# Swapping the V product and the t product on TensorE in the attention slots of a gated transformer block

## What is computed

```
q = layernorm(x) @ w_q;  k = ctx @ w_k;  v = ctx @ w_v
x = x + tanh(g_xattn) * softmax(causal(q k^T / sqrt(512))) @ v
x = x + tanh(g_ffn) * (gelu(layernorm(x) @ tern(W1)^T + b1) @ tern(W2)^T + b2)
```

## Time and profile before

| | before |
|---|---|
| runs, us | 1613.87, 1618.36, 1619.16 (median 1618.36) |
| span of the profiled execution, first to last instruction | 1614.5 us, mean granted clock of PE 0.991 |
| busy PE, DVE, ACT, POOL | 1574.7, 1087.3, 811.1, 481.5 us |
| attention stage, from 43 to 766 us | 723.0 us, PE busy 704.5, DVE busy 489.3 |

### The profile page before, as it was taken

The page is one execution under the profiler, slowest core; times in us unless marked ns, Lnnn a source line. Parts: engine busy times, 40 slices in busy tenths (PEclk is TensorE's granted clock), DMA queues, the critical chain, the costliest instruction groups (busy, mean ns, idle before and its releaser), DMA issues.

```text
span 1614.5 us, 26067 instructions
## 1 busy us (share of the span) xinstructions
PE 1574.7 (98%) x10028; PEld 982.1 (61%) x10028; DVE 1087.3 (67%) x1825; ACT 811.1 (50%) x1448; POOL 481.5 (30%) x467
## 2 busy tenths in 40 slices
PE   7799999999999999999989999999999999999998
PEld 4455556565656555555656666666666666666665
DVE  6666657665656679866666677667676677667664
ACT  2333333433233553323656666666666666666664
POOL 3211111111111111133344443345344444345320
PEclk9899999999999999999999999999999999999999
DMA  7445455453646986666222333324222323323110
GB/s 209 111 94 150 104 142 111 113 133 91 153 101 169 222 249 158 150 156 119 63 76 48 97 79 85 78 55 98 76 76 47 98 76 82 74 65 98 50 50 27
DMA packets 307532, 170.81 MB, mean 106 GB/s; under 512 B 268160, under 2 KB 268176, under 8 KB 306128
## 3 DMA queue, kind: packets, MB, share of 16 engines
q1 hardware_dynamic: 306512, 166.78, 42.2%
q10 hardware_dynamic: 720, 2.10, 0.4%
q0 software_dynamic: 176, 0.27, 0.1%
HBM read 70.53 MB, written 33.55 MB: 64 GB/s over the span
## 4 chain that ended last, share of the span: by engine, by line
PE 89%; DVE 4%; issue 2%; ACT 1%; DMA 1%; POOL 0%; SPq 0%; DVEq 0%
PE s_ps L1234 14%; PE e_ps L1234 14%; PE s_ps L1299 11%; PE o_ps L1329 10%; PE v_ps L1280 9%; PE t_ps L1261 8%; PE t_ps L1178 7%; PE o_ps L1178 7%; PE v_ps L1178 7%; PE m_ps L1178 3%; DVE w_s L1074 1%; DMA x_ring<-in_x 1%; DVE negmax L897 0%; PE e_ps L1329 0%; DVE ctx_s L742 0%
## 5 line engine op out<-in xcount | busy, mean ns | idle before, releaser
L1037 DVE SCALAR_TENSOR_TENSOR v_s<-xnT,sc,v_s 128x512 f16<-128x512 f32 x256 | 239.7, 957 | 104.7 <-ACT v_s L667 104.7
L660 ACT ACTIVATE xnT<-tT,b_s 128x256 f32<-128x256 f32 x384 | 173.9, 499 | 178.5 <-DVE tT L1025 62.2
L1234 PE MATMUL s_ps<-w_s,v_s 128*128 128x512 f16 x1024 | 262.8, 379 | 0.0
L1234 PE MATMUL e_ps<-w_s,v_s 128*128 128x512 f16 x1024 | 262.8, 379 | 0.0
L563 ACT ACTIVATE p<-s_ps,ebias,esc 128x128 f32<-128x128 f32 (+3 forms) x64 | 53.2, 831 | 355.7 <-DVE ebias L901 355.7
L1299 PE MATMUL s_ps<-ctx_s,tT 128*128 128x512 f16 (+3 forms) x1152 | 197.7, 326 | 3.7 <-DVE tT L858 3.7
L1329 PE MATMUL o_ps<-v_s,pT 128*128 128x512 f16 x840 | 192.0, 380 | 0.0
L1280 PE MATMUL v_ps<-wv_s,ctx_s 128*128 128x512 f16 x768 | 180.0, 385 | 7.8 <-DVE v_s L865 7.8
L1261 PE MATMUL t_ps<-xnT,a_s 128*128 128x256 f16 x1488 | 176.9, 276 | 8.2 <-issue 7.9
L667 ACT ACTIVATE v_s<-xnT,sc 128x512 f16<-128x512 f32 x256 | 176.2, 712 | 7.5
L1234 PEld LDWEIGHTS e_ps<-w_s,v_s 128*128 128x128 f16 x1024 | 100.2, 98 | 120.8
(11 more groups left out here) (169 smaller groups left out, 2401.5 us busy)
## 6 DMA issues: line engine op xcount, KB each, us to landing
out_y<-x_ring SPq DMA_DIRECT2D x128, 256.0 KB, 2.2
x_ring<-in_x SPq DMA_DIRECT2D x64, 256.0 KB, 3.0
raw<-in_ctxT SPq DMA_DIRECT2D x7, 2048.0 KB, 8.2
raw<-out_y SPq DMA_DIRECT2D x44, 256.0 KB, 3.8
w_in<-in_w1T SPq DMA_DIRECT2D x16, 512.0 KB, 4.3
w_in<-in_w2T SPq DMA_DIRECT2D x16, 512.0 KB, 4.4
x_ring<-out_y SPq DMA_DIRECT2D x20, 256.0 KB, 3.7
raw<-in_ctxT SPq DMA_DIRECT2D x2, 1024.0 KB, 16.3
```

What stands on the lines that cost most here:

```text
L660: a.activation(g32n[:, j, half * 2 * P:(half + 1) * 2 * P], src, ACT.Gelu, bias=b1_s[:, f:f + 1], scale=1.0 / YN).then_inc(g_act, 1)
L1037: v.scalar_tensor_tensor(out=g_s[:, U % 2, j, LO], in0=g32n[:, j], scalar=col(C_SG), in1=g_s[:, U % 2, j, HI], op0=ALU.mult, op1=ALU.subtr ...
L1234: last_mm = mm(y_ps[i], g_s[:, U % 2, j, a, i * P:(i + 1) * P], w2_s[:, f, :], start=(U % UG == 0 and n == 0 and a == HI), stop=(U % UG == ...
```

## The change

PE makes the V product ahead of the t product in every slot. The programs of ACT, DVE, POOL and SP stay as they are, row for row.

```diff
                     last_mm.then_inc(s_mm, 1)
-                if s > 0 and (not last or t < NT - T_LEAD):
-                    t_product(it, s)
                 if last and t == NT:
 
                     unit_second(0)
...
                     unit_first(0)
                 if not last or t + 1 < NT:
                     v_product(it, s)
+                if s > 0 and (not last or t < NT - T_LEAD):
+                    t_product(it, s)
                 if t - 1 in TOTAL_SLOTS:
```

## The result

| | before | after |
|---|---|---|
| runs, us | 1616.11 (1613.34 to 1619.16, 4 runs) | 1639.86 (1638.94 to 1640.68, 4 runs) |
| ratio of the medians | | 1.0147, 95% interval 1.0134 to 1.0159 |
| span of the profiled execution | 1614.5 | 1637.8 us |
| attention, 43 us to the start of the feed-forward stage | 723.0 us, PE busy 704.48 | 746.3 us, PE busy 712.19 |
| feed-forward stage | 848.5 us, PE busy 836.92 | 848.5 us, PE busy 836.93 |

A forecast was written before the change was run, and what follows sets the result against it. PE was taken to bound the attention, busy 704.48 of 723.00 us. Terms 10.2 + 3.2 - 4.0 + 1.0 + 16.5 = 26.9 us, added to 1618.36, gave 1645 us (49%), range 1630 to 1662.

The forecast's parts named there:

- The main step: Both read-outs hang on the later end of t, since ACT reads V behind t; earlier V is worth nothing itself.
- A: Slots i = 1 to 4 of five middle sequences: late t_lower and DVE delay S, +2.03 us each, 10.2 us.
- B: Slot i = 7 into the next sequence: later reads delay V, +0.45 us, seven times, 3.2 us.
- C: First sequence: V fills PE's idle hole before t of slot 2, PV starts 4.98 us earlier; net -4.0 us.
- the give-back: Waits of slots 3 and 4 in the first sequence return part of the gain: 0.65 to 2.03, taken as 1.0 us.
- D: Sequence from t = 48: late t adds between nothing and 2.03 us where DVE is nearly always busy; +1.0 us.
- Faster: Rival: V fills a hole wherever t waits for transposed rows, slots 2 and 50, giving 1612 us; 3%.
- E: Slots 58 to 60: PE idles about 4 us before V, which then runs at half clock; +16.5 us.
- the rival of late slots at full clock: Rival: slots 58 to 60 keep full clock, costing 8.7 instead of 16.5 us, in all 1637; 22%.
- The clock did not fall in A: Rival judged: six middle sequences each make at least one V at 1.2 GHz, +15 us, 1660; 12%.
- a delay that is absorbed in the last slots: Rival: the chain through POOL does not move with t, last slots cost 2 to 5 us, 1626 to 1632; 10%.

The follow-up runs named there:

- The reads in the new order: The changed kernel with ACT and DVE also reading V before t, on DVE ahead of the ternary weights too: 1619.96 us, ratio 1.0026 to the kernel before.
- experiment at full clock in the late slots: The changed kernel plus 17 unused matmuls ahead of V in each of slots 58 to 60, filling PE's wait: 1633.74 us, against 1615.83 before the change.
- first experiment: The kernel before the change with V ahead of t only in slots 9, 17, 25, 33 and 41: 1624.89 us against 1615.65, ratio 1.0057.

## Why the prediction was right, and where it was off

- **The main step holds.** ACT starts on t 0.20 us behind the start of PV, and the earlier V is worth nothing while its read stands behind that of t. The reads in the new order show it by taking it away: the waits for V vanish outside the slots 0 and 1, and 19.4 us with them, though in the late slots the ternary weights lose their place ahead of V as well.
- **A was right**, in size (1.97 for 2.03 each) and in place. The wait before S of slot 18 costs 0.94 us for the 1.03 forecast, since S starts 0.06 us behind t_lower and not 0.15. The chain of waits of after shows "From there DVE is the bound" directly.
- **B was wrong in five of seven places.** The step that failed is "v_lower from 226.78 to 227.85", t_upper's delay of 1.07 us carried over whole. The 4.62 us from t_upper to v_lower in the earlier trace rows held a wait: t_lower started 1.26 us behind t_upper there, at 223.42, since DVE was still at the lower part of the probabilities (the two rows of before below). After the change t comes later than that work, t_lower follows at 0.63 us, and v_lower at 3.99 (220.75 to 224.74). It ends at 225.43, ahead of V of slot 16 at 225.75. 0.63 of the 1.07 us were slack, and the rest stayed below the wait. Only at t = 48 and 56, where DVE has ternary weights ahead of v_lower as well (0.75 and 2.28 us in slot 47), it costs 0.5.

```profile
222.28 1.23 DVE L915 SCALAR_TENSOR_TENSOR p_s<-p,p_s 128x1024 f16<-128x1024 f32 x1 [1.45 <-ACT p_s L568]
223.42 0.68 DVE L858 SCALAR_TENSOR_TENSOR tT<-t_ps,tT 128x512 f16<-128x512 f32 x1
```

- **C was right**: PV of slot 2 went from 75.73 to 70.06, 5.67 earlier, 4.98 of it beyond the shorter setup, the figure of the forecast; the give-back was 1.21 and not 1.0.
- **D was mis-sized**, +3.2 for +1.0. The step is "A late t product adds between nothing, where DVE is late in any case, and the 2.03 of A. I take the middle", which leaves out the clock. It also rests on a wrong reading: PE did not wait 1.48 us for DVE in the earlier trace rows. The timeline of before gives the wait to the t product of slot 50, at 604.45, with 1.44 us for "issue", as in slot 2 (the rival *Faster* reads it so), and V did not wait there. The swap filled this wait, and a wait of 2.00 us for the read-out of V came in its place. V of slot 50 ran at 0.61 and took 4.27 us. In the experiment at full clock in the late slots the same V, behind the same idle of 2.00, ran at 1.00 and took 2.58, and D was 1.26 (6.32 to 7.58). 1.7 of the 1.9 us between the two are this one product at the lower clock. The row of that experiment:

```profile
611.75 2.75 PE L1280 MATMUL v_ps<-wv_s,ctx_s 128*128 128x512 f16 x12 [2.00 <-DVE v_s L865]
```

- **E had the right mechanism, place and idles** (3.99 us for a forecast of 4.07), and its working at full clock, 8.7 us, is what the experiment at full clock measured, 8.65. Mis-sized is "I give V 5.2 us": the three took 4.28, 3.92 and 4.22. The clock cost 4.7 us, not 7.8. So 13.3 lies between the forecast and the rival of late slots at full clock, somewhat nearer to the forecast. With V first in the slots 57 to 61 alone two of the three took 5.07 and 5.03, so how near 5.2 comes to the truth differs from execution to execution. The 1.3 us that a slow V of slot 59 "already cost" before, an argument of the forecast, cost the kernel nothing: with the old order there and a V of 2.59 us (first experiment), the V of slot 60 only waits longer, 2.16 us for 1.05, and starts where it would have. V's length counts only where V is in the loop.
- **The clock did not fall in A.** Over 242.60 to 267.00 us, with idles of 0.77, 0.29 and 0.26, the granted clock of after is 1.00, and the products there keep 2.59 and 2.62 us; over 52.50 to 612.20 us, all five sequences, it is 1.00 too. The Trainium skill's rule that small idles between groups of matmuls can make the clock swing ("TensorE: Matmul & The Clock Gate", A second HAM failure mode: psum-queue depth-cycling) does not show in this stretch.
- **Faster** fell, as its own point of decision said: three matmuls do not cover 1.67 us. What was right in it is slot 2 alone, 3.6 us.
- **Two slips elsewhere.** That the chain of waits lies on PE alone holds from slot 2 to slot 47, not from 573 to 624 and from 688 to 723 us, where it lies on DVE, ACT, POOL, SP and a load. And a delay that is absorbed in the last slots (E of 2 to 5) gives 1631 to 1634 by the forecast's own sum, not 1626 to 1632.

In all 26.9 us were forecast and 23.7 measured; the time, 1639.86 for 1645, is lower by the difference and by the kernel before, whose median is 1616.11 and not 1618.36 with the fourth run. That the total came nearer than the terms is luck: B and E were 5.4 us too high together, D 2.2 too low, and how long V takes at the lower clock differs between executions.

## What to carry to other kernels

Where two products are read out by in-order engines, and the readers take first the product that now ends last, swapping the makers without the readers makes both results as late as the later one. Count from the end of the product that is read first, and look for the slot with the least work behind it. Take a duration between two instructions on a reader from a row in which neither was held by something else; a wait hidden in it (B) turns into a cost that does not exist. Here the swap paid only where PE idled ahead of one product while the other was ready: in one slot of 64, for 0.23%. And ask first whether the engine is in the chain of that stage: a slow product costs nothing beside the chain, and its whole excess in it.

## What was unexpected of the hardware

How long V takes behind an idle is not set by the idle alone. Behind 2.00 us in slot 50 it took 4.27 us in one kernel and 2.58 in another whose slot 50 is the same; behind 3.98 us in slot 59 it took 3.92 and 5.07, behind 4.54 in slot 60 4.22 and 5.03. In slot 59 with the old order, behind 2.22 to 2.23 us of idle, it took 3.84 in before, 4.12 with V first in slot 2, and 2.59 in both kernels whose swaps lie in the middle sequences; from slot 48 on these four programs are the same. What differs is how much of V lies in the stretch at the lower clock. In slot 58 of after the granted clock was 1.00 (2.4 GHz) over the first 0.56 us of V, and then 0.50 (1.2 GHz):

```profile
710.64:711.20 0.56, 0.56 (x3) 0.29 (x4) 0.53 (x2) 0.00 (x0) 0.00 (x0) 1.00 0.00 0
711.30:714.60 3.30, 3.30 (x9) 1.22 (x8) 3.09 (x11) 1.29 (x3) 0.55 (x1) 0.50 0.42 119
```

In slot 59 of the kernel with V first in the slots 57 to 61 it was 0.50 over all of V. So the clock can fall when PE is already at work again. Each number comes from one profiled execution, so these runs don't tell a difference between kernels from one between executions. The Trainium skill ("TensorE: Matmul & The Clock Gate", What's actually happening) says that the watch over PE's activity runs freely and does not start with the kernel, so that the same kernel's slow matmuls differ in number from run to run; the pairs of rows fit that, but nothing here shows the cause.
